# A sorted mixture-of-experts stage: slots of one expert and 256 rows, or of two chunks of 128 rows

## The reference

```
logits = xf @ router_w.T + experts_bias
rw, sel = top_k(logits, 2);  rw = softmax(rw)
g = einsum('td,edh->teh', xf, w1);  u = einsum('td,edh->teh', xf, w3)
moe_out = einsum('te,teh,ehd->td', cw, silu(g) * u, w2)      # cw: rw of the two chosen experts, else 0
shared_out = (silu(xf @ sw1) * (xf @ sw3)) @ sw2
x = x + 0.5 * (moe_out + shared_out)
```

## Time and profile before

| | us |
|---|---|
| median of 3 runs | 1103.01 (1101.13 to 1104.15) |
| the profiled execution | 1102.1 |
| its span, first to last instruction | 1100.1 |
| busy: PE / DVE / POOL / ACT | 947.3 / 850.5 / 676.0 / 656.4 |
| the second mixture of experts in the span | about 686 to 829 |
| its 39 slots' matmuls | 706.7 to 811.8 |

### The profile page before, as it was taken

One profiled execution on the slowest core, in us unless ns is written; L12 is line 12 of the kernel. 1 busy time (PEld: TensorE's weight loads), 2 busy tenths in 40 slices (PEclk: granted clock), 3 DMA queues, 4 the chain that ended last, 5 costly groups with the idle time before them and its releaser, 6 DMA issues. The chain is left out here.

```text
span 1100.1 us, 30497 instructions
## 1 busy us (share of the span) xinstructions
PE 947.3 (86%) x10944; PEld 717.1 (65%) x10944; DVE 850.5 (77%) x2291; ACT 656.4 (60%) x1264; POOL 676.0 (61%) x722
## 2 busy tenths in 40 slices
PE   1776999589999998889999996899985999999998
PEld 1444788356767666667666664688983766666686
DVE  6885788467888878688888874899878967888872
ACT  4753565547777776667677754456654664343574
POOL 4878553465565585856765524567772328899852
PEclk9997999799999999899999997899997999999999
DMA  8314452333433343433333321633214000000011
GB/s 239 111 52 111 139 146 80 68 50 61 66 61 61 57 81 53 79 59 64 67 66 60 60 46 43 197 91 106 84 51 152 2 1 1 1 1 1 1 30 48
DMA packets 279953, 75.54 MB, mean 69 GB/s; under 512 B 217312, under 2 KB 273792, under 8 KB 279424
## 3 DMA queue, kind: packets, MB, share of 16 engines
q1 hardware_dynamic: 270816, 53.50, 23.9%
q0 software_dynamic: 8992, 20.11, 5.8%
HBM read 28.15 MB, written 24.17 MB: 48 GB/s over the span
## 5 line engine op out<-in xcount | busy, mean ns | idle before, releaser
L2961 DVE TENSOR_REDUCE diff_peak<-diff_s_ps 128x2 f16<-128x384 f32 (+7 forms) x384 | 208.5, 558 | 69.5 <-PE diff_s_ps L3210 65.6
L2844 ACT ACTIVATE diff_prob<-diff_st_ps 128x512 f32<-128x512 f32 x320 | 186.4, 595 | 90.0 <-PE diff_st_ps L3232 87.7
L3210 PE MATMUL diff_s_ps<-diff_down_or_kT,diff_up_or_block 128*128 128x32 f16 (+7 forms) x1024 | 129.4, 228 | 0.0
L3232 PE MATMUL diff_st_ps<-diff_qT,diff_rows_or_pair 128*128 128x256 f16 (+3 forms) x1024 | 123.6, 234 | 0.0
L1007 ACT ACTIVATE moe_h_hi<-moe_h 128x512 f16<-128x512 f32 x94 | 59.2, 630 | 89.9 <-DVE moe_h L1417 89.7
L3248 PE MATMUL diff_ot_ps<-diff_prob,diff_v 128*32 128x256 f32 (+3 forms) x2048 | 109.7, 308 | 0.4 <-ACT diff_prob L2844 0.4
L3207 PE MATMUL diff_s_ps<-diff_mask,diff_ident_bf 128*128 128x64 bf16 (+1 forms) x384 | 79.0, 206 | 28.8 <-DVE diff_peak L2961 19.3
L868 POOL DMA_INDIRECT exp_ys<-moe_y_sb,moe_dest x78 | 79.4, 1019 | 33.3 <-issue 20.0
L3528 POOL TENSOR_TENSOR lin_y<-lin_state,lin_qT 128x512 f32<-128x512 f32 x64 | 81.2, 1268 | 16.8 <-DVE lin_state L3692 14.1
L3692 DVE TENSOR_TENSOR_SCAN lin_state<-banks_all,lin_kv 128x512 f32<-128x512 f32 x64 | 76.9, 1216 | 15.3 <-POOL lin_kv L3521 13.4
L844 POOL DMA_INDIRECT exp_xs<-diff_rows_or_pair,exp_rows x64 | 66.7, 1041 | 23.7 <-issue 18.8
(11 more groups left out here) (495 smaller groups left out, 2952.0 us busy)
## 6 DMA issues: line engine op xcount, KB each, us to landing
moe_xg<-exp_xs SPq DMA_DIRECT2D x78, 130.0 KB, 2.4
diff_up_or_block<-diff_qT SPq DMA_DIRECT2D x128, 64.0 KB
diff_rows_or_pair<-diff_down_or_kT SPq DMA_DIRECT2D x128, 64.0 KB, 2.1
exp_y_slots<-moe_y_sb SPq DMA_DIRECT2D x39, 128.0 KB, 2.2
diff_v_new<-diff_v_raw SPq DMA_DIRECT2D x64, 64.0 KB
fetched_yg<-exp_ys SPq DMA_DIRECT2D x7, 512.0 KB, 4.5
all_x<-in_x SPq DMA_DIRECT2D x4, 512.0 KB, 5.2
diff_up_or_block<-in_w SPq DMA_DIRECT2D x16, 128.0 KB, 3.8
```

Source lines behind the costliest of these rows:

```text
L2844: nc.scalar.activation(prob[:, n % RING], st_ps[:, e % 2], ACT.Exp, scale=SCALE).then_inc(exp_ready, 1)
L2961: nc.vector.tensor_reduce(peak[:, half, c0:c0 + n, i], s_ps[:, u % 2, 0:n * wd].rearrange("p (c k) -> p c k", k=wd), op=ALU.max, axis=AX.X ...
L3210: last = nc.tensor.matmul(out[:, c], q_block[:, ch, i].rearrange("p r q -> p (r q)"), kT[:, B % 2, ch, 0:wd], start=False, stop=True, skip ...
L3232: last = nc.tensor.matmul(out[:, at:at + wd], k_pair[:, h % 2, h // 2, i].rearrange("p r k -> p (r k)"), qT[:, C % 3, h // 2, KB * i:S], s ...
```

## The change

In the second stage alone, a slot of 256 rows becomes two chunks (HS = 2) of CH = 128 rows, each with an expert of its own. Experts are padded to 128 rows, so 71 chunks are needed at most, and NS = 36 slots (72 chunks) are processed in place of 39; FULL becomes 24. The first stage has CH = 256, HS = 1 and NS = 39, as before. The tables have an entry for each chunk. SP fetches a slot with two loads into registers and two DMAs of 128 rows. The up product becomes 24 matmuls of 128 columns; the down product has as many matmuls as before, its second half with the second chunk's expert. The address step L1402 becomes two instructions.

```diff
+    CH = P if ahead else SLOT
+    HS = SLOT // CH
+    NS = (2 * NT * P // CH + E - 1 + HS - 1) // HS
+    NCH = NS * HS
+    FULL = max(0, -(-(2 * full_groups * GN - E * (CH - 1)) // CH)) // HS
+    FULL_CH = FULL * HS
+    slot_row = ew.slot_row[:, 0:SLOTS * SLOT // P:CH // P]
...
-    for s in range(SLOTS):
+    for s in range(NS):
...
             def fetch_rows(s):
-                row = sp.value_load(row_tab[0:1, s:s + 1], min_val=0, max_val=E * REGION + P * PAD - SLOT)
+                if HS == 1:
+                    starts = [sp.value_load(row_tab[0:1, s:s + 1], min_val=0, max_val=E * REGION + P * PAD - CH)]
+                else:
+                    _, starts = nc.values_load_multi_w_load_instructions(
+                        row_tab[0:1, s * HS:s * HS + HS], engines=[mybir.EngineType.SP], min_val=0, max_val=E * REGION + P * PAD - CH)
...
-                sp.dma_start(xg[:, s % XR], ew.xs[bass.ds(row, SLOT)].rearrange("(j p) d -> p j d", p=P)).then_inc(row_in[s % XR], 16)
+                for n, row in enumerate(starts):
+                    tiles = slice(n * J // HS, (n + 1) * J // HS)
+                    sp.dma_start(xg[:, s % XR, tiles], ew.xs[bass.ds(row, CH)].rearrange("(j p) d -> p j d", p=P)).then_inc(row_in[s % XR], 16)
...
             def count_full_slots():
-                nslots = NT * P // SLOT
+                nslots = NT * P // CH
...
                 for part in range(3):
-                    fill_tables(slice(0, FULL), part)
+                    fill_tables(slice(0, FULL_CH), part)
...
                 words = xg[:, s % XR, :, 2 * P:].bitcast(F32)
-                step(nc.vector.scalar_tensor_tensor(place[:, s % 2], words[:, :, 0], own_region[:, s:s + 1], words[:, :, 1],
-                                                    ALU.not_equal, ALU.add))
+                for j in range(J):
+                    c = s * HS + j * HS // J
+                    last = nc.vector.scalar_tensor_tensor(place[:, s % 2, j:j + 1], words[:, j, 0:1], own_region[:, c:c + 1], words[:, j, 1:2],
+                                                          ALU.not_equal, ALU.add)
+                step(last)
...
             def expert_up(s):
                     for c in range(NC):
-                        for n, (wt, part) in enumerate(((ew.up_hi, 0), (ew.up_hi, 1), (ew.up_lo, 0))):
-                            lhs = wt[:, bass.ds(e, 1), which, c * P:(c + 1) * P].rearrange("p a b -> p (a b)")
-                            last = nc.tensor.matmul(ps[:, i % 2, c * SLOT:(c + 1) * SLOT], lhs, xgT[:, s % 2, part],
-                                                    start=(n == 0), stop=(n == 2))
+                        for half in range(HS):
+                            e, tokens = experts[s * HS + half], slice(half * CH, (half + 1) * CH)
+                            out = ps[:, i % 2, c * SLOT + half * CH:c * SLOT + (half + 1) * CH]
+                            for n, (wt, part) in enumerate(((ew.up_hi, 0), (ew.up_hi, 1), (ew.up_lo, 0))):
+                                lhs = wt[:, bass.ds(e, 1), which, c * P:(c + 1) * P].rearrange("p a b -> p (a b)")
+                                last = nc.tensor.matmul(out, lhs, xgT[:, s % 2, part, tokens], start=(n == 0), stop=(n == 2))
...
             def expert_down(s):
-                e = experts.pop(s)
+                of = [experts.pop(s * HS + half) for half in range(HS)]
...
-                            rhs = wp[:, bass.ds(e, 1), c].rearrange("p a d -> p (a d)")
+                            rhs = wp[:, bass.ds(of[j * HS // J], 1), c].rearrange("p a d -> p (a d)")
```

More of the change, by code:

```diff
@@ L645, in sorted_moe @@
             gone_of = nm.sb("gone_of", [P, E], F16)
-            here = nm.sb("here", [P, SLOTS], F16)
+            here = nm.sb("here", [P, NCH], F16)
             early = nm.sb("early", [P, E], F32)
@@ L798, in _ @@
                         n_stored += 1
-                for n in range(n_stored, SLOTS):
+                for n in range(n_stored, NS):
                     store_rows(n)
@@ L803, in _ @@
                 for i in range(YR):
-                    sp.wait_ge(y_stored[i], 16 * len(range(i, SLOTS, YR)))
+                    sp.wait_ge(y_stored[i], 16 * len(range(i, NS, YR)))
                 sp.wait_ge(opening.v_dup_in, 64)
@@ L817, in _ @@
                 for i in range(YR):
-                    sp.wait_ge(y_stored[i], 16 * J * len(range(i, SLOTS, YR)))
+                    sp.wait_ge(y_stored[i], 16 * J * len(range(i, NS, YR)))
             if fetched_here:
@@ L1197, in make_full_tables @@
                 step(nc.vector.tensor_tensor(before[:], upto[:], slots_of[:], ALU.subtract))
-                nc.vector.tensor_scalar(taken[:, 0:E], upto[:], float(FULL * SLOT), None, ALU.min)
-                step(nc.vector.tensor_scalar(before[:], before[:], float(FULL * SLOT), None, ALU.min))
+                nc.vector.tensor_scalar(taken[:, 0:E], upto[:], float(FULL_CH * CH), None, ALU.min)
+                step(nc.vector.tensor_scalar(before[:], before[:], float(FULL_CH * CH), None, ALU.min))
                 nc.vector.memset(taken[:, E:], 0.0)
@@ L1253, in find_slots @@
                 step(nc.vector.tensor_copy(position[:], position_ps))
-                n = SLOTS - FULL if late else FULL
-                step(nc.vector.tensor_scalar(slot_at[:, 0:n], ew.slot_row[:, 0:n], 1.0 / SLOT, None, ALU.mult))
+                n = NS - FULL if late else FULL
+                step(nc.vector.tensor_scalar(slot_at[:, 0:n], slot_row[:, 0:n], 1.0 / SLOT, None, ALU.mult))
                 nc.vector.tensor_scalar(here[:, 0:n], slot_at[:, 0:n], position[:, 0:1], usable[:, late:late + 1], ALU.is_equal, ALU.mult).then_inc(slots_found, 1)
@@ L1264, in number_slots @@
                 dve.wait_ge(numbers_in_psum, 2 * late + 2)
-                slots = slice(FULL, SLOTS) if late else slice(0, FULL)
+                slots = slice(FULL, NS) if late else slice(0, FULL)
                 n = slots.stop - slots.start
@@ L1661, in experts_from @@
             def experts_from(s):
-                if s in experts:
+                c = s * HS
+                if c in experts:
                     return
@@ L1852, in _ @@
                 opening.transpose_queries(pe, 1)
-            pe.wait_ge(y_ready, SLOTS)
+            pe.wait_ge(y_ready, NS)
 class Fetched:
```

61 lines of the change are left out of this document (30 added, 31 removed).

## The result

The changed kernel takes **1135.38 us** (median of 4 runs, 1132.35 to 1138.77), the kernel before beside it 1103.58: the ratio is 1.0295, 95% interval 1.0255 to 1.0334. Five more runs of the same kernel in a later job gave 1133.34 (1.0294, 1.0275 to 1.0313). The forecast was 1121 with a range of 1105 to 1134: the direction was right, the size 14 us too small, the time just above the range. The profiled execution took 1138.77 (span 1137.0).

What follows compares the result with a forecast made beforehand. PE and POOL bound the stage before; PE's sequencer would after the change. Tables 0.9, first to last up 19.4, last up 0.6 and end -2.8 sum to +18.1 us: median 1121 us, range 1105 to 1134.

Steps and rivals of the forecast that it cites:

- The sequencer becomes the bound: PE in the second stage's slots: 24 register instructions, waits and loads take 3.38 us per slot against 2.2 of array.
- rival A: Second stage's slots: sequencer hides the register instructions, array stays the bound at 2.2 us per slot, total 1097; chance 8%.
- C: Second stage's slots: worse than the sum, through a granted clock falling to 1.2 GHz or long loads, total 1133; chance 14%.
- B: Up or down product: fewer register instructions, 20 or 16 per slot instead of 24; with 20, total 1105; chance 10%.
- The period, 3.38 us: PE's sequencer per slot: 24 register instructions at 0.118 us, three waits 0.34, load 0.20; 33 periods make 111.5 us.
- The load, 0.20 per slot: Load of experts' numbers on PE's sequencer, every second slot: median 0.34 us and gap, 0.40, long loads left out.
- First two slots: Start of the slots, with shared items multiplied down without register instructions: 2.43 us each, 4.9 for both.
- Shared items, 0.5 each: Four shared items between slots: waits plus what the queue can't lend, 2.0 us together; bounds 0.34 and 1.4 each.
- Last up to the last shared addition: Behind the last up's start: the last slot's up takes 1.9 us in place of 1.3, +0.6.
- Tables, +0.9: Table steps on DVE before the slots: four steps on 384 elements in place of 168, nothing hides it; bounds 0.5 and 1.3.
- The end, -2.8: End of the stage: DVE's waits for fetched results go, as POOL finishes during six shared items; bounds 0 and -2.8.
- Address step and fetches, nothing: Second address instruction on DVE, at most 0.21 us per slot, hidden; SP's extra row fetches 0, bound 1.

Runs made afterwards that it cites:

- b_24x: Kernel before with up as 24 matmuls of 128 columns, experts' numbers loaded twice, 24 register instructions per slot, 39 slots: 1138.66 us, ratio 1.0352.
- a_fixed: Changed kernel with the second stage's experts fixed at build time, so no register instructions or loads of experts' numbers there: 1102.49 us, ratio 1.0016.
- a_none: Changed kernel with no shared item between its slots, ten behind the last slot: 1141.65 us, ratio 1.0385.
- a_eight: Changed kernel with eight shared items between the slots and two behind: 1129.0 us, ratio 1.0268.
- a_shift192: Changed kernel with slot_row 88 floats wide, so all tensors behind it lie 192 bytes after their old place: 1125.65 us, ratio 1.0219.
- a_again: The changed kernel run again, unchanged: 1133.34 us, ratio 1.0294.
- a_layout: Changed kernel with slot_row in float16, putting every tensor but the second stage's own back in its old place: 1128.09 us, ratio 1.0236.
- b_lay2: Kernel before with slot_row 78 floats wide, half unused, all tensors behind it 160 bytes later; repeat for more runs: 1109.2 us, ratio 1.008.
- b_late: Kernel before with 160 unused bytes behind the class's tensors, so only the stages' own tensors move: 1109.68 us, ratio 1.0072.
- b_layout: Kernel before with slot_row 78 floats wide, half unused, all tensors behind it 160 bytes later: 1112.06 us, ratio 1.011.
- b_shift32: Kernel before with slot_row 47 floats wide, tensors behind it 32 bytes later: 1105.25 us, ratio 1.0036.
- b_down2: Kernel before with experts' numbers loaded twice and a second register in down's second half, 16 register instructions per slot: 1107.79 us, ratio 1.0076.

## Why the prediction came out as it did

The direction and the mechanism in the stage were right. The time is 32 us up, not 18, for two reasons: the stage's sum had one term too small (5.8 of the 14 us), and the sum had no term at all for the wider `slot_row`, which costs the rest in the attention.

- **The sequencer becomes the bound: right.** The count (24 register instructions, 288 FUSED_REGOPS, 18 loads), the group of three at 0.24 us, the gaps ended by "issue", POOL waiting for ACT, and the clock of 1.00 are all as forecast. Rivals A and C fell in the trace of the changed kernel, and B with the count. b_24x and a_fixed show the cause from both sides, though each changes the loads of experts' numbers too (7.2 us in b_24x).
- **The period, 3.38 us: too small, 3.555 (a_none).** The step that failed is the size of a register instruction: 0.118 was read from one short stretch of the earlier trace rows, which had no long spacing in it; the average is 0.1248. Of the 0.175 us that a slot takes more, 24 x 0.0068 = 0.16 are this term, the rest waits and loads. 33 x 0.175 = +5.8. This is the whole excess of the stretch (124.25 against 118.4 us), since the next two nearly cancel.
- **The load, 0.20 per slot: right by luck.** I left the long loads out because they stood "where the sequencer is ahead of the array". b_24x has long loads with the sequencer as the bound. They stayed away here because of where the changed kernel's loads begin in the table, as far as these traces show.
- **First two slots: too cheap.** They were forecast at 2.43 each; up to up they take 2.78 and 3.33 in the second trace of the changed kernel (6.1 together for 4.9): +1.2.
- **Shared items, 0.5 each: too dear.** a_none, the changed kernel and a_eight give 0.25 to 0.33: -0.7 to -1. That is close to the waits alone (0.34), which the prediction gave as the reading by the Trainium skill ("TensorE: Matmul & The Clock Gate", section "Architectural detail: the array is 16× 32×32, not 1× 128×128", by its queue of 64). Its cost agrees; the depth itself no run shows. Limiting the queue to the lead of 0.97 us seen before was my error: a lead seen where the array is the bound is not the queue's capacity.
- **Last up to the last shared addition: +0.6 forecast, +1.0 measured** (19.07 against 18.11).
- **Tables, +0.9: +0.7** at the first slot's up. The four steps take 0.55 each, near 0.32 + 0.21 as forecast; 710.02 is the first.
- **The end, -2.8: right.** The additions wait for no DMA. a_eight shows the other side: with two items behind the slots there is a wait of 7.7 us.
- **Address step and fetches, nothing: right** as far as the trace shows; the address takes 0.42 us per slot, and no wait of the slots' matmuls on DVE grew (0.7 us in all before the up matmuls, 1.4 in the kernel before).
- **What was missed altogether: the attention.** This step took the time out of the range. Everything outside the second stage was put at nothing without a word, though the diff widens `slot_row`; the prediction had no term, bound or rival for it. The stage alone would have given 1101 + 24 = 1125, within the range. The other 8 us come from the tensors' place: 7.7 by a_shift192 against a_again, 5.2 by a_layout against a_again, 8 to 10 by b_lay2, b_late and b_layout. That a_shift192 measures 1125.65 is partly chance, since its stage took 168.2 and not 166; a_layout, which moves nothing ahead of the stage, is at 1128, and 2 to 3 us of that are not explained.
- **Two sums of the ranges.** The upper end of the forecast's own range adds four shared items at 0.9 more (3.6) and half of the long loads (6.8), which gives 1131, not 1128. And the 1116 beside rival A leaves the four shared items out. Neither bears on the result.

Left open: which wait of the attention turns slower packets into time (the traces show longer packets, and a chain in which many engines take part); why b_shift32 costs 4 us and b_lay2 8 at the same queue share (the packets of 512 bytes differ, 33.4 against 39.3 ns, but no run tried them alone); and the last 4 us of the profiled execution's attention (480.3, against 476.3 in the second trace), which are within what runs of one kernel differ by. The attentions of the kept traces overlap, so how the 8 us spread inside it can't be read from them. Whether a load's beginning in the table makes it long wasn't tried either.

## What to carry to other kernels

Before an operand's address is made to depend on one more register, count the register instructions per array work: below the array's pace they cost next to nothing (16 per slot in b_down2), above it each costs its spacing (here 0.125 us, the rare long ones included), and a busy share of 86% shows neither. Take a rate for a bound from the longest stretch that has it, not from the cleanest: the small stalls are part of it. And look at each line of a change for what it moves: a tensor that lives through the whole program and grows by a few bytes shifts all behind it, and when DMAs reach those, keep the shift a multiple of 64.

## What the runs showed that I had not expected

- Register instructions on PE's sequencer have a steady spacing of 0.124 and 0.113 us, whatever the matmuls between, with a stall of 0.15 us about every 8 us, by the estimate above 256 instructions apart; 15 such stalls stand in 125 us of the changed kernel's trace.
- A load of four experts' numbers takes 0.33 us when it begins at slot 4, 8, 12 or 16 of the table, and 1.0 to 1.2 when it begins at slot 21, 25, 29 or 33, whether the array is the bound (the kernel before) or the sequencer (b_24x).
- DMA packets take 11% more time for the same bytes when the tensors they reach in SBUF start 32 bytes beyond a multiple of 64 (29.9 to 30.2% against 33.3 to 33.6% of the engines' time, in 8 and 9 traces), and the whole kernel 0.4 to 1.1% more. A packet of 64 bytes takes 9.0 ns against 10.0 to 10.3.
- Matmuls of 128 columns with weights of their own follow each other in 0.056 us also in a row of 24 (784.91 to 786.25 above).
